# An attention and FFN kernel: the copy of the largest tile of turned probabilities goes from ScalarE to VectorE

## The reference

```
x: (4, 512, 512)   16 heads of 32   FFN 512 -> 2048 -> 512
xn = layernorm(x)
q, k, v = xn @ Wq + bq, xn @ Wk + bk, xn @ Wv + bv          # per head
scores = q k^T / sqrt(32) + slope[h] * (key - 511), causal
ctx = softmax(scores) @ v
out = x + (ctx @ Wo + bo) + ffn(xn)
ffn(t) = (silu(t @ gate^T) * (t @ up^T)) @ down^T, its weights cubic splines of control points
```

## Time and profile before

| what | value |
|---|---|
| median of 3 runs | 739.25 us (739.19 to 741.35) |
| the profiled execution | 739.71 us |
| its span, first to last instruction | 737.9 us |
| PE busy | 665.9 us (90%) |
| VectorE busy | 458.3 us (62%) |
| ScalarE busy | 452.7 us (61%) |
| GpSimd busy | 322.6 us (44%) |
| mean granted clock of TensorE | 0.984 |

### The profile page before, as it was taken

How to read it: one execution, slowest core, us unless ns; L and a number is a source line. 1 busy time by engine, 2 the same in 40 slices (tenths; PEclk the granted TensorE clock), 3 DMA queues, 4 the chain that set the end, 5 groups by cost and what they waited for, 6 DMA issues and landing times.

```text
span 737.9 us, 13725 instructions
## 1 busy us (share of the span) xinstructions
PE 665.9 (90%) x4884; PEld 535.3 (73%) x4884; DVE 458.3 (62%) x1287; ACT 452.7 (61%) x729; POOL 322.6 (44%) x188
## 2 busy tenths in 40 slices
PE   4977889989799898899897787878999999999997
PEld 3766668777678776678676675657888888888885
DVE  6757867879877879778799897674441213213112
ACT  5487987877977878878879863543533333333331
POOL 0264654544654544544545520321253245236334
PEclk9997999999999999999999999998999999999999
DMA  8769387476676384963956959865666475244001
GB/s 315 109 86 249 52 262 129 67 136 169 92 209 87 44 130 101 225 90 45 214 87 83 389 183 263 231 211 167 173 207 217 122 238 167 64 147 151 2 1 57
DMA packets 53355, 110.15 MB, mean 149 GB/s; under 512 B 6504, under 2 KB 6760, under 8 KB 51752
## 3 DMA queue, kind: packets, MB, share of 16 engines
q1 hardware_dynamic: 52984, 108.95, 60.3%
q10 hardware_dynamic: 304, 0.33, 0.2%
HBM read 59.32 MB, written 25.17 MB: 114 GB/s over the span
## 4 chain that ended last, share of the span: by engine, by line
PE 42%; POOL 4%; issue 4%; DVE 3%; SPq 3%; DMA 2%; ACT 1%; POOLq 0%; DVEq 0%; ACTq 0%
PE bank L1607 7%; PE bank L1609 6%; PE bank L1608 6%; PE bank L704 3%; PE bank L1594 3%; PE bank L1595 3%; POOL resid L1772 3%; PE bank L616 2%; PE bank L690 2%; DMA wgu_lo<-wgu_lo 2%; PE bank L618 2%; PE bank L617 2%; SPq L330 2%; POOL in_lo L1764 1%; PE bank L721 1%
## 5 line engine op out<-in xcount | busy, mean ns | idle before, releaser
L1259 POOL TENSOR_TENSOR work<-work 128x1280 f16<-128x1280 f32 x64 | 170.8, 2669 | 168.2 <-ACT work L1153 168.2
L1764 POOL TENSOR_TENSOR in_lo<-inner,in_hi 128x512 fp32r<-128x512 f32 x64 | 83.2, 1302 | 195.3 <-ACT in_hi L1674 195.3
L907 DVE CUSTOM_DVE_ANT_0 work<-bank,dist 128x128 f32<-128x128 f32 (+3 forms) x256 | 115.3, 486 | 61.7 <-PE bank L690 45.0
L1145 ACT ACTIVATE work<-work,neg_max 128x128 f32<-128x128 f32 (+3 forms) x256 | 128.7, 561 | 11.2 <-DVE neg_max L907 11.0
L1722 DVE TENSOR_TENSOR inner<-bank,silu 128x512 f32<-128x512 f32 x64 | 44.0, 688 | 134.0 <-ACT silu L1668 134.0
L1674 ACT CAST in_hi<-inner 128x512 fp32r<-128x512 f32 x64 | 39.7, 621 | 136.4 <-PE bank L1609 136.4
L704 PE MATMUL bank<-ident,work 128*128 128x128 f16 x1280 | 105.4, 225 | 13.4 <-ACT work L1160 6.7
L704 PEld LDWEIGHTS bank<-ident,work 128*128 128x128 f16 x1280 | 74.9, 100 | 50.0 <-issue 31.3
L1153 ACT CAST work<-work 128x1280 f16<-128x1280 f32 x64 | 80.6, 1259 | 47.9 <-PE bank L704 47.2
L1607 PE MATMUL bank<-w_room,in_hi 128*128 128x512 f32 x256 | 100.0, 390 | 0.7 <-POOL in_lo L1764 0.7
L1608 PE MATMUL bank<-w_room,in_hi 128*128 128x512 f32 x256 | 99.6, 389 | 0.0
(11 more groups left out here) (114 smaller groups left out, 1302.5 us busy)
## 6 DMA issues: line engine op xcount, KB each, us to landing
q_stack<-parts SPq DMA_DIRECT2D x48, 256.0 KB, 5.8
k_stack<-parts SPq DMA_DIRECT2D x48, 256.0 KB, 6.5
z<-xt_scratch SPq DMA_DIRECT2D x128, 88.0 KB
x_in<-x SPq DMA_DIRECT2D x32, 256.0 KB, 6.7
xt_scratch<-xt_room SPq DMA_DIRECT2D x8, 1024.0 KB, 7.9
xt_room<-xt_scratch SPq DMA_DIRECT2D x6, 1024.0 KB, 8.6
factor<-c_basis SPq DMA_DIRECT2D x5, 1024.0 KB, 11.0
taps<-windows SPq DMA_DIRECT2D x5, 1024.0 KB, 13.8
```

Source lines behind the costliest of these rows:

```text
L907: dve.tensor_tensor_reduce(probs[:, s % 2, OFF[i]:OFF[i] + n], score_bank[i % 2][:, 0:n], dist[:, S - n:S], -slope(s), 3.4e38, ALU.add, AL ...
L1145: e = act.activation(tile, tile, ACT.Exp, bias=neg_max[:, s % 2, i:i + 1], scale=-1.0)
L1259: pool.tensor_tensor(probs16[:, s % 2, 1, :], probs[:, s % 2, :], probs16[:, s % 2, 0, :], ALU.subtract).then_inc(lo_ready, 1)
L1764: pool.tensor_tensor(in_lo[k % 2][:, :], inner[:, k % 2, :], in_hi[:, k % 2, :].bitcast(F32), ALU.subtract).then_inc(il_ready, 1)
```

## The change

In `attention_vector`, `step` now calls `take_turned` for tile 3 as well, directly behind tile 2. In `attention_scalar` the function `take_turned` and its call are gone. VectorE's own `take_turned` is as it was; it waits for the weighing of the head before last at tile 0 only, which stands for the later tiles too.

```
--- before.py
+++ after.py
@@ attention_vector, step @@
             if turned:
                 take_turned(*turned, 2)
+                take_turned(*turned, 3)
             for of, (kind, n) in turns if s not in (3, 11) else []:
                 (x_low if kind == "x" else ctx_low)(of, n)
@@ attention_scalar @@
-        def take_turned(b, s, i):
-            n = 2 * (i + 1) * P
-            act.wait_ge(pt_full, 4 * (H * b + s) + i + 1)
-            if later(b) or s >= 2:
-                act.wait_ge(av_full, H * b + s - 1)
-            act.copy(probs_t[:, s % 2, 2 * OFF[i]:2 * OFF[i] + n],
-                     pt_bank[i % 2][:, 0:n]).then_inc(pt_free[i % 2], 1)
-
@@ attention_scalar, step @@
                 probs_high(b, s)
-            if turned:
-                take_turned(*turned, 3)
             for key in units_at(b, s, carry):
```

## The result

The changed kernel takes 832.98 us (median of 4 runs, 830.71 to 835.81) against 739.22 us before; the ratio is 1.126, with a 95% interval of 1.124 to 1.129. The forecast was 826 us, the range 783 to 846. The profiled execution took 832.71 us, 93.0 more than the one before. Up to the end of the last turn it is 97.2 us longer (536.5 for 439.3 us from the start of the span); what comes behind is 4.2 us shorter (294.4 for 298.6).

A forecast was written before the change was run, and what follows sets the result against it. The prediction took PE and VectorE, waiting for each other in turns, to bound the head loop. Its sum was 739.7 + 20 (copy) + 30 (clear holds) + 27 (knife's edge) + 9 (clock) = 826 us, range 783 to 846.

The forecast's parts named there:

- The copy: Head loop: 64 VectorE copies move VectorE by 0.61 us each, less cover and 1.4 us regained in step 10: +20 us.
- take 3: The copy of turned tile 3 out of PSUM, moved from ScalarE to VectorE; forecast to last 0.69 us.
- Clear holds: Thirteen places where VectorE's pushed two-SBUF-input instructions start behind GpSimd's and are held until it ends: +30 us.
- (b,1): Step 1 of batch b: L897, 0.39 us ahead of GpSimd, comes 0.22 behind and is held, 2.3 us.
- (b,13): Step 13 of batch b: the hold is hidden by the step's cover but for 0.3 us.
- (b,2): Step 2 of batch b: L897 comes 0.14 us behind GpSimd, L895 too if ScalarE casts sooner; held 2.3 us.
- Knife's edge: Steps 4, 5, 6, 14: L897 lands 0.02 to 0.03 us behind GpSimd; eleven places at 2.47 us, +27 or nothing.
- turn 3: The PE transposes that fill turned tile 3 in PSUM; GpSimd's L1259 starts 1.43 us after they end.
- The clock: PE runs slower after long waits: 0.73 us for about half of 24 places, +9 us, bounds 0 and 20.
- Behind the heads: Everything after the head loop waits for the last turn and moves along, with no term of its own.
- only the clear cases: Rival: the knife's edge places are not held, 795 us; chance 0.27.
- No holds: Rival: only the 0.61 us per step is added, no VectorE instruction is held, 760 us; chance 0.07.

The follow-up runs named there:

- the kernel with 960 columns: Changed kernel with VectorE's copy of turned tile 3 cut to 960 of 1024 columns: 792.33 us, ratio 1.071.
- the kernel in which GpSimd waits: Changed kernel, but GpSimd waits, before its low part, until VectorE has finished the split of v of the step before: 767.85 us, ratio 1.038.
- the kernel with added turning: Changed kernel, but in steps behind a split of v PE turns tile 0 before scores tile 2, twelve times instead of once: 827.74 us, ratio 1.119.

## Why the prediction was right, and where it was not

The mechanism and its place were right. That the sum came within 7 us of the time is partly luck: of the four terms one had about the right size, the two of the holds together were a quarter too large, the clock was far too small, and the part behind the heads, which was to move along unchanged, became shorter. These errors partly cancelled.

- **The copy, +20.** Right in size. It lasts 0.682 us and moves a step by 0.60. A batch without holds is 4.5 us longer (forecast 4.6) with take 3 behind the split, and 6.5 in the order of the change, with its time at 1.2 GHz. The forecast took back 0.45 us in each step 10; the kernel with the copy in step 9 alone shows 0.6, all that the copy had cost in step 9.
- **Clear holds, +30.** Ten of thirteen places came. (b,1) is 2.3 us longer three times, L895 in (1,2) and (3,2) is held 2.3 us longer than its own time, steps 4 to 7 of the last batch have five holds, (3,15) has one of 2.1 us, and (b,13) gives little. But (0,5) and (2,2) were free, L897 being 8 and 5 ns ahead, and nothing was held in (3,9). By the step lengths some 25 us. For (b,2) the prediction reckons with VectorE pushed back and names ScalarE's earlier cast only as a condition. That half, GpSimd coming forward because ScalarE no longer copies in step 1, is enough alone in two of three batches.
- **Knife's edge, +27.** Eight of eleven places were held, at 2.49 us by the steps ((2,14): 8.63 with it, 6.14 in the kernel with 960 columns): 20 us. The prediction took one value, +0.024, for all. In truth there are two. GpSimd starts 1.43 us after turn 3 ends in all of them, so the order hangs on when take 3 starts: where it has to queue behind take 2 it starts 0.065 us after turn 3 ends, and L897 lands 10 to 20 ns behind; where it starts 0.038 us after turn 3's end, L897 lands 3 to 8 ns ahead. Which of the two it is was not traced back further.
- **The clock, +9, bounds 0 to 20.** This is the term that was mis-sized. The mean granted clock fell from 0.984 over 737.9 us to 0.929 over 830.9: by (1 - clock) x span x 2, from 24 to 118 us at 1.2 GHz. What the other terms leave of the 97.2 us up to the last turn is 97 - 20 - 25 - 20 = 32 us. I priced a stretch at 0.73 us, what one row of 14 transposes lost, and thought of half of 24 places. A stretch lasts 3.4 us or a multiple of that and covers matmuls and scores too; where two like steps differ in it, it costs 1.5 to 1.7 us. The 32 is a remainder, not a measurement of its own.
- **Behind the heads, 0.** "Everything behind the heads waits for the last turn and moves along": it moved, but is 4.2 us shorter, with less waiting of PE before the FFN's gate matmuls. No experiment was made on it.
- **The range.** It is said to go from the clear cases with no loss to the clock to all cases with the full one. By the terms that is 739.7 + 20 + 30 = 790 to 739.7 + 20 + 30 + 27 + 20 = 837; the 783 and 846 stand 7 and 9 us outside, and no row gives these. The measured time lies in the narrower range as well.

The sum of the two hold terms was 12 us too high, the clock 23 too low, and 4 us came back behind the heads. The Trainium skill (SBUF — State Buffer, "Who interferes with whom") names the lock and says that who issues first keeps it; the runs agree, with L897 held from 8 ns behind on, and its rule that a copy with one SBUF input at most stays out of it, outside the two-port modes, fits the take out of PSUM that overlapped GpSimd and kept its 0.68 us. It names casts among those that can use two ports, which would cover L895; no run here shows its mode.

Of the signs that were to show it: take 3 at 0.69 us, yes; a batch with all holds 19 to 22 us longer, batches 1 and 2 are 28.2 and 22.7 longer, the lost clock included; L897 in (b,1) near 2.7, it is 2.75; L895 in (b,2) near 2.6, in two of three; L897 in (b,5) either way, both occur. PE's waits for the maxima were to be about 90 us; they are 63.5. Fewer places were held, and PE's wait in (2,4) and ten more held steps is 2.6 us and not the 2.9 of the prediction; that PE at half clock works through a part of them is likely but not shown.

Of the rivals, "only the clear cases" (795 us) is near the kernel with 960 columns, at 792, in which the edge cases are free (but (1,2) and (3,2) too). "No holds" (760) is near the kernel in which GpSimd waits, 768. Not settled is how the 32 us of clock divide over the places, and why, with the copy left out in step 1, L898 lands 141 and 151 ns behind GpSimd in (1,2) and (2,2) but 1 ns ahead in (3,2).

## What to carry to other kernels

Before work is added to VectorE, list its instructions whose inputs are in SBUF and how far ahead of the next GpSimd instruction each starts: where that lead is smaller than what is added, the price is up to GpSimd's whole duration, not the added time (here 2.3 to 2.5 us a place for 0.6 added). A semaphore by which GpSimd starts last cost little here, where its result was not due, and removed the hold (833 to 768 us), but look at what GpSimd now starts ahead of instead. Relieving an engine that feeds GpSimd can do the same harm from the other side, so an engine that is less busy is no gain in itself.

## What the runs showed of the hardware that was not expected

- The order of two starts decides at a distance of a few nanoseconds. L897 with a recorded start 10 ns or more behind GpSimd's was always held (8 ns in the kernel with added turning); 3 ns behind and 3 ns ahead it was free. 34 ns less in the copy ahead were worth 40 us.
- The cast L895, with one input in SBUF (fp32 to bf16, 0.29 us), is held as the subtractions are, 2.58 us, behind the low part. Beside GpSimd's small L1238 (128x2, 0.8 us) it took its 0.29. The copies out of PSUM and the biases of scores in PSUM never were held.
- A held instruction ends sooner after GpSimd than its own length: L897 at 312.35 + 2.88 ends 0.28 us behind GpSimd's end at 312.34 + 2.61, not 0.43; L343 at 528.12 + 2.82 ends 0.55 behind, not 0.68.
- Each fall of PE to 1.2 GHz in the loop of the changed kernel, for 3.4 us or twice that, came behind a wait of 1.1 us or more. Not every such wait had one: behind 2.59 us in (2,6) PE stayed at 2.4 GHz. In the steps compared, a stretch at 1.2 GHz cost 1.5 to 1.7 us.
